# Attention scores from one fp32 copy of the queries and keys instead of fp16 halves

## The chip, the cores and the metric

One core of a Trainium2 chip runs the whole kernel. The metric is the time on the device of one execution, in microseconds (us); smaller is better. TensorE (PE) multiplies, with its weight loads recorded apart (PEld); VectorE (DVE), ScalarE (ACT) and GpSimd (POOL) do the elementwise work, and SyncE (SP) issues the DMAs.

## The reference

The reference is a decoder layer for 32 batches of 112 rows by 256 columns: attention with 8 heads of 128, a gelu block whose weights are the batch's own 375 context rows, and a quantised feed-forward block with 1024 hidden units. Each block has a layer norm in front and a residual behind. The part that changes is the scores of the attention:

```python
q = jnp.einsum('bim,mhd->bhid', x, wq)
k = jnp.einsum('bim,mhd->bhid', x, wk)
...
q = _rmsnorm(q)
k = _rmsnorm(k)
q = _rope(q)
k = _rope(k)
...
s = jnp.einsum('bhid,bhjd->bhij', q * mult, k * mult)
...
p = jax.nn.softmax(s, axis=-1)
o = jnp.einsum('bhij,bhjd->bhid', p, v)
```

## The kernel before

**Tiling.** One batch is one step of a software pipeline. All weights stay in SBUF. In step `i` each engine works on batch `a` = i (projections of q, k and v, rotary turn and norms), `b` = i-1 (scores, softmax, values, output projection), `c` = i-2 (context block and hidden units) and `d` = i-3 (the last product and the store). The order in a step is written out by hand for each engine, in the function `body` of each engine's block; every engine takes its instructions strictly in that order, and semaphores tie the engines together. The first three steps (`FIRST`, `SECOND`, `THIRD`) also split and transpose the weights, and the last three drain the pipeline.

**Precision.** Several products are made of two halves of each operand, a rounded one (`_hi`) and the rest (`_lo`): `split_products` (lines 872 to 877) issues hi times hi, hi times lo and lo times hi into one accumulation. The projections, the output projection and the context product use `F32R` halves. The scores use fp16 halves. The products of the probabilities with the values (`weigh_values`, line 937) and of the context with the normalised rows (`ctx_hidden`, line 982) take plain fp32 operands, one `pe.matmul` call each.

**The scores of batch `b`.** PE transposes the 8 heads of q and of k into PSUM (`transpose_qk`, line 917: `qT_ps` in banks 0 and 1, `kT_ps` in banks 2 and 3). ACT copies each into `qkT_hi` as fp16 (`split_qkT`, lines 710 to 713; the copy itself is recorded under line 684). DVE subtracts that copy from the same PSUM and writes `qkT_lo` (`split_qkT`, lines 548 to 552). PE waits for both `lo` copies, then makes three products of 128 by 112 by 112 a head (`scores`, lines 921 to 929, recorded under line 876). They go to `s_ps`, in banks 0 and 1 again. ACT takes the exponential (line 728), POOL masks it (line 367).

**The order around them.** On PE a step runs: transposes of q and k (b), projection of q (a, line 909), `out_units` (d, line 1013), transposes of the normalised rows `xn2` (c, line 965), scores (b), `ctx_hidden` (c, line 982), projection of k (a), transposes of the context (b, line 972; they wait for the exponential), `weigh_values` (b), `ctx_out` (c), projection of v in two halves with the transposes of the attention output between them (line 944), the transposes for the next step, then the output projection (b, line 876) with `hidden_units` (c, line 1005) between its parts. On DVE a step begins with the two subtractions, with `normalise_x2` (c, line 468) between them (behind both in the last steps), then `residual_out` (d, line 577), which waits for `out_units`. In `THIRD` there is also `split_wo(0)` (line 463) between the two subtractions. On ACT a step begins with the two copies (in `THIRD` the copy `wo_hi` stands between them), then `square_qk` (line 718).

The mapping of calls to matmul records matters below: in a trace every record on PE has its own weight load on PEld.

Of the kernel before, what the change touches and what calls it, by code (L numbers as in the profile page):

```python
# [22 lines left out]

F32 = mybir.dt.float32
F16 = mybir.dt.float16
F32R = mybir.dt.float32r
BF16 = mybir.dt.bfloat16
I16 = mybir.dt.int16
# [1 line left out]
ALU = mybir.AluOpType  # L30
AX_X = mybir.AxisListType.X

P = 128
# [35 lines left out]
def done(j):  # L69

    return j.base + j.off + 1
# [12 lines left out]
def decoder_layer(nc, x, ctx_rows, wq, wk, wv, wo, w1, b1, w2, b2, tables, out):  # L84
    B, T, M = x.shape
    S = ctx_rows.shape[1]
    _, H, D = wq.shape
# [6 lines left out]
    HH = H // 2  # L94
# [5 lines left out]
    with ExitStack() as stack:  # L100
        def sb(name, shape, dt=F32):
            return stack.enter_context(nc.sbuf_tensor(name, shape, dt))

        def sem(name):
            return stack.enter_context(nc.semaphore(name))
# [53 lines left out]
        ms = sb("ms", [T, 2, H])  # L159
        rms = sb("rms", [T, 2, H])  # L160
        qkn = sb("qkn", [T, 2, HD])
        qkT_hi = sb("qkT_hi", [P, 2, H * T], F16)
        qkT_lo = sb("qkT_lo", [P, 2, H * T], F16)
        v_sb = sb("v_sb", [T, H, VW])
        rden = sb("rden", [T, H])
        oT_hi = sb("oT_hi", [P, H, T], F32R)
# [25 lines left out]
        def bank(n, width, dt=F32):  # L192
            return psum[:, n, 0:width] if dt == F32 else psum[:, n, :].bitcast(dt)[:, 0:width]

        qT_ps, kT_ps = psum[:, 0:2, 0:HH * T], psum[:, 2:4, 0:HH * T]
        q_ps, k_ps, v_ps = psum[0:T, 4:6, :], psum[0:T, 2:4, :], psum[0:T, 0:2, :]
        s_ps = psum[0:T, 0:2, 0:HH * T]
# [26 lines left out]
            "xnT_ready", "q_ready", "k_ready", "v_ready", "qT_ready", "kT_ready", "s_ready", "o_ready"))  # L224
        oT_ready, y_ready, xn2T_ready, ctxT_ready, h_ready, ctxout_ready, xqT_ready, f_ready, f2_ready = map(sem, (
            "oT_ready", "y_ready", "xn2T_ready", "ctxT_ready", "h_ready", "ctxout_ready", "xqT_ready", "f_ready", "f2_ready"))
        xnT_hi_done, q_squared, k_squared, v_copied, qT_hi_done, kT_hi_done = map(sem, (
            "xnT_hi_done", "q_squared", "k_squared", "v_copied", "qT_hi_done", "kT_hi_done"))
        qT_lo_done, kT_lo_done = sem("qT_lo_done"), sem("kT_lo_done")
        exp_done, p_done, oT_hi_done, xn2T_copied, ctxT_copied, h_squared, tanh_done, xqT_copied, f_int_done = map(sem, (  # L230
            "exp_done", "p_done", "oT_hi_done", "xn2T_copied", "ctxT_copied", "h_squared", "tanh_done", "xqT_copied", "f_int_done"))
        stat_done = [sem(f"stat_done{n}") for n in range(3)]
# [165 lines left out]
        def _(dve):  # L398
# [18 lines left out]
            def x_rows(j):  # L417
                return 0, x_in[:, j.off % SLOTS, :], j
# [4 lines left out]
            def wait_x(j):  # L423
                dve.wait_ge(x_landed[j.off % SLOTS], landed(j))
# [41 lines left out]
            def normalise_x2(j):  # L466
                dve.wait_ge(rstd_done[1], done(j))
                dve.tensor_scalar(xn2[:, :], x2[:, j.off % 2, :], mv[1][:, 0:1], rstd[1][:, 0:1],
                                  ALU.subtract, ALU.mult).then_inc(xn2_done, 1)
# [75 lines left out]
                dve.wait_ge(xq_int_done, done(j))  # L545
                fixed(xq[:, :], xq_int[:, :]).then_inc(xq_done, 1)

            def split_qkT(w, j):
                dve.wait_ge((qT_hi_done, kT_hi_done)[w], done(j))
                dve.tensor_tensor(qkT_lo[:, w, :].rearrange("p (b n) -> p b n", b=2), (qT_ps, kT_ps)[w],  # L550
                                  qkT_hi[:, w, :].rearrange("p (b n) -> p b n", b=2),
                                  ALU.subtract).then_inc((qT_lo_done, kT_lo_done)[w], 1)

            def split_oT(n, j):
                dve.wait_ge(oT_hi_done, half(j, n))
                hs = slice(n * HH, (n + 1) * HH)
# [23 lines left out]
            def body(i):  # L580
                a, b, c, d, n, m = i, i.plus(-1), i.plus(-2), i.plus(-3), i.plus(1), i.plus(2)
                A, B_, C, D_, N, M_ = (j.inside(B) for j in (a, b, c, d, n, m))
                if i is FIRST:
                    wait_x(n)
                    layer_stats(x_rows(n))
                    normalise_x(n)
                    split_xnT(n)
                    for w in range(3):
                        split_projection(w)
                    dve.wait_ge(ident_in, 16)  # L590
                    dve.tensor_copy(ident_b[:, :], ident[:, :]).then_inc(ident_b_done, 1)
                    wait_x(m)
                    layer_stats(x_rows(m))
                    return
                if i is SECOND:
                    normalise_x(n)
                    dve.wait_ge(table_in, 32)
                    turn_cos(0, a)
                    turn_sin(0, a)
                    sum_squares(0, a).then_inc(q_summed, 1)  # L600
                    split_xnT(n)
                    turn(0, a)
                    sum_squares(1, a).then_inc(k_summed, 1)
                    turn_cos(1, a)
                    turn_sin(1, a)
                    turn(1, a)
                    normalise_k(a)
                    clip_weights(0)
                    return
                if B_:  # L610
                    split_qkT(0, b)
                if i is THIRD:
                    split_wo(0)
                if C and A:
                    normalise_x2(c)
                if B_:
                    split_qkT(1, b)
                if C and not A:
                    normalise_x2(c)
                if i is THIRD:  # L620
                    wait_x(n)
                    layer_stats(x_rows(n))
                    clip_weights(1)
                    fixed_biases()
                if D_:
                    residual_out(d)
                if A:
                    turn_cos(0, a)
                    turn_sin(0, a)
                    sum_squares(0, a).then_inc(q_summed, 1)  # L630
                if C:
                    gelu_inner(c)
                if N:
                    normalise_x(n)
                if C:
                    gelu_outer(c)
                if A:
                    turn(0, a)
                if C:
                    split_g(c)  # L640
                if A:
                    turn_cos(1, a)
                if B_:
                    invert_sums(b)
                if A:
                    turn_sin(1, a)
                if i is THIRD:
                    split_wo(1)
                if C:
                    residual_ctx(c)  # L650
                if A:
                    sum_squares(1, a, slice(0, HH))
                if B_:
                    split_oT(0, b)
                if C:
                    quantise_x3(c)
                if A:
                    sum_squares(1, a, slice(HH, H)).then_inc(k_summed, 1)
                if B_:
                    split_oT(1, b)  # L660
                if A:
                    turn(1, a)
                if N:
                    split_xnT(n)
                if A:
                    normalise_k(a)
                if B_:
                    residual_attention(b)
                if M_:
                    wait_x(m)  # L670
                if B_:
                    dve.wait_ge(x2_done, done(b))
                if B_ or M_:
                    layer_stats(*([x2_rows(b)] if B_ else []), *([x_rows(m)] if M_ else []))
                if C:
                    clip_hidden(c)
# [5 lines left out]
        def _(act):  # L682
            def copy(dst, src):
                return act.activation(dst, src, ACT.Copy)  # L684
# [22 lines left out]
                       w2T[:, :, :].rearrange("p (b c) m -> p b (c m)", b=2))[n]  # L707
                copy(dst, psum[:, 6:8, :].bitcast(BF16)).then_inc(wT_copied, 1)

            def split_qkT(w, j):  # L710
                act.wait_ge((qT_ready, kT_ready)[w], done(j))
                copy(qkT_hi[:, w, :].rearrange("p (b n) -> p b n", b=2),
                     (qT_ps, kT_ps)[w]).then_inc((qT_hi_done, kT_hi_done)[w], 1)

            def square_qk(w, j):

# [85 lines left out]
            def body(i):  # L802
                a, b, c, d, n, m = i, i.plus(-1), i.plus(-2), i.plus(-3), i.plus(1), i.plus(2)
                A, B_, C, D_, N, M_ = (j.inside(B) for j in (a, b, c, d, n, m))
# [12 lines left out]
                    round_weights(1)  # L817
                    return
                if B_:
                    split_qkT(0, b)  # L820
                if i is THIRD:
                    split_wo()
                if B_:
                    split_qkT(1, b)
                if i is THIRD:
                    copy_wT(0)
                if A:
# [43 lines left out]
        def _(pe):  # L871
            def split_products(dst, pairs, first=True, last=True):

                terms = [(lh, rh) for l, r in pairs for lh, rh in ((l[0], r[0]), (l[0], r[1]), (l[1], r[0]))]
                for k, (lh, rh) in enumerate(terms):
                    product = pe.matmul(dst, lh, rh, start=first and k == 0, stop=last and k == len(terms) - 1)  # L876
                return product
# [42 lines left out]

            def scores(j):

                pe.wait_ge(qT_lo_done, done(j))
                pe.wait_ge(kT_lo_done, done(j))
                for h in range(H):
                    at = slice(h * T, (h + 1) * T)
                    last = split_products(s_ps[:, h // HH, (h % HH) * T:(h % HH + 1) * T],
                                          [((qkT_hi[:, 1, at], qkT_lo[:, 1, at]), (qkT_hi[:, 0, at], qkT_lo[:, 0, at]))])
                last.then_inc(s_ready, 1)

            def weigh_values(j):
# [194 lines left out]
```

## Time and profile before

| what | value |
|---|---|
| time, median of 3 runs | 747.37 us |
| the runs | 747.22, 747.37, 750.02 us |
| span of the profiled execution, first to last instruction | 745.4 us |
| the profiled execution's own time | its span; no other time is listed for it |
| what the median has beyond the span | 1.97 us (0.3%) |
| PE, PEld busy | 96%, 85% |
| DVE, ACT, POOL busy | 88%, 74%, 41% |
| mean granted clock of TensorE | 0.985 of full |

A row of a group of instructions gives line, engine, operation, the tiles written and read, and the shapes. For a matmul "128*112 128x512" is a stationary operand (the weights that are loaded) of 128 rows and 112 columns, and a moving operand of 128 rows and 512 columns. Matmuls overlap in the pipeline, so the duration of one (over 200 ns) is not what it costs in a stream; the distance from one start to the next is, and so is the time that a group takes in the chain of waits divided by its count. The ends of matmuls are modelled, so small waits can hide in a PE that looks fully busy.

### The profile page before, as it was taken

How to read it: one execution, taken by the hardware profiler on the slowest of the kernel's cores; microseconds unless marked ns; L12 is line 12 of the kernel's file. 1: busy time of each engine (PE TensorE's matmuls, PEld its weight loads, DVE VectorE, ACT ScalarE, POOL GpSimd, SP SyncE). 2: the span in 40 equal slices, each digit the busy share in tenths (PEclk: the TensorE clock that was granted, in tenths of full speed). 3: DMA queues.
4: the chain of work that ended last, by engine and by line, in shares of the span. 5: the costliest groups of instructions: out<-in, count | busy, mean ns of one | idle time of the engine just before them, and what ended most of it. 6: DMA issues, size and time to landing. Idle time of an engine off the chain costs nothing.

```text
span 745.4 us, 15919 instructions
## 1 busy us (share of the span) xinstructions
PE 714.9 (96%) x5824; PEld 633.9 (85%) x5824; DVE 655.2 (88%) x1264; ACT 548.8 (74%) x1324; POOL 308.1 (41%) x425
## 2 busy tenths in 40 slices
PE   5799999999999999999999999999999999999974
PEld 4588988888888989898898989889898988889863
DVE  6989989999999999999999999999999999998942
ACT  5777777778777777787777878777787777778752
POOL 1335434543443453344344344444434444443421
PEclk9799999999999999999999999999999999999996
DMA  7400011100101100000110000101000011100000
GB/s 264 157 8 28 28 36 34 31 17 28 33 27 33 33 24 21 27 31 29 33 33 19 26 27 27 33 33 33 15 30 27 27 33 34 33 11 20 28 7 12
DMA packets 15371, 26.58 MB, mean 36 GB/s; under 512 B 1536, under 2 KB 10192, under 8 KB 15216
## 3 DMA queue, kind: packets, MB, share of 16 engines
q1 hardware_dynamic: 15344, 26.22, 10.7%
q8 instruction: 17, 0.28, 0.2%
q14 instruction: 10, 0.08, 0.0%
HBM read 22.55 MB, written 3.67 MB: 35 GB/s over the span
## 4 chain that ended last, share of the span: by engine, by line
PE 90%; DVE 3%; ACT 3%; issue 2%; DMA 1%; POOL 1%; SPq 0%; POOLq 0%; DVEq 0%; ACTq 0%
PE psum L909 34%; PE psum L876 22%; PE psum L937 7%; PE psum L917 6%; PE psum L982 6%; PE psum L1013 4%; PE psum L1005 3%; PE psum L944 3%; PE psum L972 3%; PE psum L965 2%; DMA w_raw<-in_wv 1%; ACT qkn L774 1%; ACT w_raw L764 1%; PE psum L997 1%; DVE qkT_lo L550 0%
## 5 line engine op out<-in xcount | busy, mean ns | idle before, releaser
L909 PE MATMUL psum<-wqkv_hi,xnT_hi 128*112 128x512 f32 x384 | 159.3, 415 | 4.4 <-DVE wqkv_lo L440 2.7
L909 PE MATMUL psum<-wqkv_lo,xnT_hi 128*112 128x512 f32 x384 | 151.3, 394 | 0.0
L909 PE MATMUL psum<-wqkv_hi,xnT_lo 128*112 128x512 f32 x384 | 131.8, 397 | 0.0
L344 POOL TENSOR_TENSOR rstd<-ve,nhalf 112x1 f32<-112x1 f32 x96 | 55.4, 577 | 145.8 <-DVE ve L414 140.8
L351 POOL TENSOR_TENSOR rms<-ms,nhalf 112x8 f32<-112x8 f32 x64 | 107.2, 1676 | 5.0
L718 ACT ACTIVATE sq<-psum 112x1024 f32<-112x1024 f32 x64 | 65.0, 1016 | 56.4 <-PE psum L909 56.4
L355 POOL TENSOR_TENSOR ctx_lo<-ctx_in,ctx_hi 125x768 fp32r<-125x768 f32 x32 | 58.6, 1830 | 95.9 <-ACT ctx_hi L684 95.9
L764 ACT ACTIVATE w_raw<-psum,rden 112x128 f32<-112x128 f32 x256 | 69.7, 384 | 26.6 <-DVE rden L525 26.5
L909 PEld LDWEIGHTS psum<-wqkv_hi,xnT_lo 128*112 128x112 f32 x384 | 67.3, 175 | 22.4
L909 PEld LDWEIGHTS psum<-wqkv_hi,xnT_hi 128*112 128x112 f32 x384 | 67.7, 176 | 19.8 <-issue 3.1
L774 ACT ACTIVATE qkn<-turn_c,rms 112x128 f32<-112x128 f32 x256 | 81.5, 400 | 1.4 <-POOL rms L351 1.4
L474 DVE TENSOR_REDUCE ss<-sq 112x4 f32<-112x512 f32 (+1 forms) x95 | 81.8, 861 | 0.0
L909 PEld LDWEIGHTS psum<-wqkv_lo,xnT_hi 128*112 128x112 f32 x384 | 67.9, 177 | 15.1
L482 DVE TENSOR_TENSOR turn_c<-psum,cos_t 112x1024 f32<-112x1024 f32 x64 | 77.8, 1216 | 2.2 <-ACT sq L718 2.2
L876 PE MATMUL psum<-wo_hi,oT_hi 128*112 128x256 f32 x256 | 78.8, 308 | 0.8 <-DVE oT_lo L557 0.8
L498 DVE TENSOR_TENSOR turn_c<-turn_c,turn_s 112x1024 f32<-112x1024 f32 x64 | 77.9, 1217 | 0.1
L491 DVE TENSOR_TENSOR turn_s<-psum,sin_t 112x1024 f32<-112x1024 f32 x64 | 77.3, 1208 | 0.0
L876 PE MATMUL psum<-wo_lo,oT_hi 128*112 128x256 f32 x256 | 72.1, 282 | 0.0
L876 PE MATMUL psum<-wo_hi,oT_lo 128*112 128x256 f32 x256 | 71.8, 281 | 0.0
L550 DVE TENSOR_TENSOR qkT_lo<-psum,qkT_hi 128x896 f16<-128x896 f32 x64 | 69.2, 1082 | 0.2 <-ACT qkT_hi L684 0.2
L788 ACT ACTIVATE f_int<-psum,b_col 128x112 int16<-128x112 f32 x256 | 65.9, 371 | 1.8 <-PE psum L1005 1.8
L937 PE MATMUL psum<-v_sb,w_raw 112*112 112x129 f32 x512 | 62.0, 273 | 0.0
(99 smaller groups left out, 1792.2 us busy)
## 6 DMA issues: line engine op xcount, KB each, us to landing
ctx_in<-in_ctx_rows SPq DMA_DIRECT2D x32, 375.0 KB
x_in<-in_x SPq DMA_DIRECT2D x32, 112.0 KB, 2.0
out_y<-y_out SPq DMA_DIRECT2D x32, 112.0 KB, 1.9
w_raw<-in_w SPq DMA_DIRECT2D x2, 1024.0 KB, 6.2
w_raw<-in_wq SPq DMA_DIRECT2D x2, 512.0 KB, 4.5
w_raw<-in_wk SPq DMA_DIRECT2D x2, 512.0 KB, 6.1
w_raw<-in_wv SPq DMA_DIRECT2D x2, 512.0 KB, 7.8
w_raw<-in_wo SPq DMA_DIRECT2D x1, 1024.0 KB, 10.3
```

The source lines that it names most:

```text
L351: pool.tensor_tensor(rms[:, w, :], ms[:, w, :], nhalf[:, 0:H], ALU.pow).then_inc(qk_rms_done[w], 1)
L474: return dve.tensor_reduce(ss[:, w, hs], heads(sq[:, w, :])[:, hs, :], AX_X, ALU.add)
L482: dve.tensor_tensor(turn_c[:, w, :].rearrange("t (b h d) -> t b h d", b=2, d=D), (q_ps, k_ps)[w].rearrange("t b (h d) -> t b h d", d=D), c ...
L491: dve.tensor_tensor(turn_s[:, w, :].rearrange("t (h two f) -> t h two f", two=2, f=HALF), halves, table, ALU.mult).then_inc(sin_done[w], 1)
L498: dve.tensor_tensor(turn_c[:, w, :], turn_c[:, w, :], turn_s[:, w, :], ALU.add).then_inc(qk_turned[w], 1)
L550: dve.tensor_tensor(qkT_lo[:, w, :].rearrange("p (b n) -> p b n", b=2), (qT_ps, kT_ps)[w], qkT_hi[:, w, :].rearrange("p (b n) -> p b n", b=2),
L764: last = act.activation(on[:, h * D:(h + 1) * D], o_ps[:, h // OH, (h % OH) * VW:(h % OH) * VW + D], ACT.Copy, scale=rden[:, h:h + 1])
L774: last = act.activation(qkn[:, 0, h * D:(h + 1) * D], turn_c[:, 0, h * D:(h + 1) * D], ACT.Copy, scale=rms[:, 0, h:h + 1])
L788: last = act.activation(f_int[:, c * T:(c + 1) * T], f_ps[:, c // (FC // 2), (c % (FC // 2)) * T:(c % (FC // 2) + 1) * T], ACT.Relu, bias= ...
L876: product = pe.matmul(dst, lh, rh, start=first and k == 0, stop=last and k == len(terms) - 1)
L909: last = pe.matmul(ps[:, n, :], left[:, c, :], right[:, c, w, n * BANK:(n + 1) * BANK], start=c == 0 and left is xnT_hi and right is wqkv_ ...
L937: last = pe.matmul(o_ps[:, h // OH, at:at + VW], p_sb[:, h * T:(h + 1) * T], v_sb[:, h, :], start=h % OH == 0, stop=h % OH == OH - 1 or h ...
```

## The change

The two fp16 tiles become one fp32 tile of the same size in bytes. ACT's copy writes fp32. DVE's subtractions go, and with them their semaphores; PE waits for ACT's copies instead. Each head's three fp16 products become one fp32 `pe.matmul` call. On DVE `normalise_x2` becomes the first instruction of a step.

```diff
-        qkT_hi = sb("qkT_hi", [P, 2, H * T], F16)
-        qkT_lo = sb("qkT_lo", [P, 2, H * T], F16)
+        qkT = sb("qkT", [P, 2, H * T])
...
-            def split_qkT(w, j):
-                dve.wait_ge((qT_hi_done, kT_hi_done)[w], done(j))
-                dve.tensor_tensor(qkT_lo[:, w, :].rearrange("p (b n) -> p b n", b=2), (qT_ps, kT_ps)[w],
-                                  qkT_hi[:, w, :].rearrange("p (b n) -> p b n", b=2),
-                                  ALU.subtract).then_inc((qT_lo_done, kT_lo_done)[w], 1)
...
-                if B_:
-                    split_qkT(0, b)
                 if i is THIRD:
                     split_wo(0)
-                if C and A:
-                    normalise_x2(c)
-                if B_:
-                    split_qkT(1, b)
-                if C and not A:
+                if C:
                     normalise_x2(c)
...
-            def split_qkT(w, j):
+            def copy_qkT(w, j):
                 act.wait_ge((qT_ready, kT_ready)[w], done(j))
-                copy(qkT_hi[:, w, :].rearrange("p (b n) -> p b n", b=2),
-                     (qT_ps, kT_ps)[w]).then_inc((qT_hi_done, kT_hi_done)[w], 1)
+                copy(qkT[:, w, :].rearrange("p (b n) -> p b n", b=2),
+                     (qT_ps, kT_ps)[w]).then_inc((qT_copied, kT_copied)[w], 1)
...
             def scores(j):
 
-                pe.wait_ge(qT_lo_done, done(j))
-                pe.wait_ge(kT_lo_done, done(j))
+                pe.wait_ge(qT_copied, done(j))
+                pe.wait_ge(kT_copied, done(j))
                 for h in range(H):
                     at = slice(h * T, (h + 1) * T)
-                    last = split_products(s_ps[:, h // HH, (h % HH) * T:(h % HH + 1) * T],
-                                          [((qkT_hi[:, 1, at], qkT_lo[:, 1, at]), (qkT_hi[:, 0, at], qkT_lo[:, 0, at]))])
+                    last = pe.matmul(s_ps[:, h // HH, (h % HH) * T:(h % HH + 1) * T],
+                                     qkT[:, 1, at], qkT[:, 0, at], start=True, stop=True)
                 last.then_inc(s_ready, 1)
```

## Rows read from the trace of the kernel before

**Rows 1.** The page's first part: engine, busy us (share of the span), instructions.

```profile
PE 714.9 (96%) x5824; PEld 633.9 (85%) x5824; DVE 655.2 (88%) x1264; ACT 548.8 (74%) x1324; POOL 308.1 (41%) x425
```

**Rows 2.** Stretches: length, PE, PEld, DVE, ACT, POOL busy (count), PE clock, DMA, GB/s.

```profile
0.00:56.00 56.00, 42.06 (x264) 34.36 (x265) 44.45 (x68) 38.61 (x59) 15.02 (x29) 0.91 0.40 143
56.00:699.00 643.00, 643.00 (x5312) 574.36 (x5311) 589.41 (x1145) 487.47 (x1204) 281.12 (x381) 1.00 0.09 28
699.00:745.40 46.40, 29.82 (x253) 25.20 (x251) 21.35 (x53) 22.70 (x63) 11.96 (x16) 0.86 0.03 8
```

**Rows 3.** The chain that ended last, one period: start us, us, what.

```profile
360.44 1.24 PE psum L876 x24
361.68 1.36 PE psum L982 x12
...
366.47 1.77 PE psum L937 x16
...
376.92 1.53 PE psum L917 x16
...
382.31 1.24 PE psum L876 x24
```

**Rows 4.** Groups on PE and DVE: shapes, count, busy us, mean ns, idle before.

```profile
L937 PE MATMUL psum<-v_sb,w_raw 112*112 112x129 f32 x512 | 62.0, 273 | 0.0
L917 PE MATMUL psum<-ident,qkn 112*128 112x112 f32 x512 | 56.2, 263 | 2.6 <-ACT qkn L774 2.2 <-DVE qkn L503 0.3
L982 PE MATMUL psum<-xn2T,ctxT 128*125 128x112 f32 x384 | 48.7, 277 | 1.6 <-issue 1.6
...
L550 DVE TENSOR_TENSOR qkT_lo<-psum,qkT_hi 128x896 f16<-128x896 f32 x64 | 69.2, 1082 | 0.2 <-ACT qkT_hi L684 0.2
```

**Rows 5.** Timeline around one batch's scores (ACT, DVE, PE): start us, us, instruction.

```profile
377.72 1.76 ACT L684 ACTIVATE qkT_hi<-psum 128x896 f16<-128x896 f32 x2
380.32 1.08 DVE L550 TENSOR_TENSOR qkT_lo<-psum,qkT_hi 128x896 f16<-128x896 f32 x1
382.16 0.42 DVE L577 SCALAR_TENSOR_TENSOR y_out<-psum,x3b 112x256 f32<-112x256 f32 x1 [0.76 <-PE psum L1013]
381.95 0.36 PE L965 MATMUL psum<-ident,xn 112*128 112x112 f32 x2
382.15 0.21 PE L876 MATMUL psum<-qkT_hi 128*112 128x112 f16 x1
383.59 0.92 ACT L728 ACTIVATE w_raw<-psum 112x896 f32<-112x896 f32 x1
```

**Rows 6.** An fp32 copy on ACT: count, shortest, median, longest ns.

```profile
L684 ACT ACTIVATE ctxT<-psum x32: 778/790/791, 40.5 to 715.5; 128x750 f32<-128x750 f32 x32
```

**Rows 7.** Timeline of the first scores (PE, ACT).

```profile
27.87 1.73 PE L917 MATMUL psum<-ident,qkn 112*128 112x112 f32 x8 [0.35 <-DVE qkn L503]
29.39 1.91 PE L885 MATMUL psum<-ident_b,w_raw 128*128 128x128 bf16 x16
32.68 0.31 PE L876 MATMUL psum<-qkT_hi 128*112 128x112 f16 x1 [1.38 <-DVE qkT_lo L550]
34.94 1.75 PE L895 MATMUL psum<-ident_b,w_raw 128*128 128x128 bf16 x16
30.18 0.91 ACT L684 ACTIVATE qkT_hi<-psum 128x896 f16<-128x896 f32 x1
```

**Rows 8.** Stretches around the first scores, columns as in rows 2.

```profile
30.00:34.00 4.00, 2.62 (x27) 2.38 (x25) 3.61 (x9) 3.75 (x4) 0.75 (x2) 0.50 0.00 0
34.00:38.00 4.00, 4.00 (x36) 3.67 (x35) 3.97 (x7) 2.34 (x3) 1.50 (x3) 0.71 0.02 4
```

**Rows 9.** Timeline of the last scores (PE, ACT).

```profile
706.52 1.08 PE L1013 MATMUL psum<-w2T,f_q 128*112 128x256 bf16 x8 [0.19 <-DVE f_q L564]
708.79 0.23 PE L876 MATMUL psum<-qkT_hi 128*112 128x112 f16 x1 [1.19 <-DVE qkT_lo L550]
705.52 1.78 ACT L684 ACTIVATE qkT_hi<-psum 128x896 f16<-128x896 f32 x2
```

More of the change, by code:

```diff
@@ L24 @@
 F32 = mybir.dt.float32
-F16 = mybir.dt.float16
 F32R = mybir.dt.float32r
@@ L226, in decoder_layer @@
             "oT_ready", "y_ready", "xn2T_ready", "ctxT_ready", "h_ready", "ctxout_ready", "xqT_ready", "f_ready", "f2_ready"))
-        xnT_hi_done, q_squared, k_squared, v_copied, qT_hi_done, kT_hi_done = map(sem, (
-            "xnT_hi_done", "q_squared", "k_squared", "v_copied", "qT_hi_done", "kT_hi_done"))
-        qT_lo_done, kT_lo_done = sem("qT_lo_done"), sem("kT_lo_done")
+        xnT_hi_done, q_squared, k_squared, v_copied, qT_copied, kT_copied = map(sem, (
+            "xnT_hi_done", "q_squared", "k_squared", "v_copied", "qT_copied", "kT_copied"))
         exp_done, p_done, oT_hi_done, xn2T_copied, ctxT_copied, h_squared, tanh_done, xqT_copied, f_int_done = map(sem, (
@@ L819, in body @@
                 if B_:
-                    split_qkT(0, b)
+                    copy_qkT(0, b)
                 if i is THIRD:
@@ L823, in body @@
                 if B_:
-                    split_qkT(1, b)
+                    copy_qkT(1, b)
                 if i is THIRD:
```

## The prediction

> **What bounds the kernel now.** I read the busy shares first: PE 96% and DVE 88% [rows 1]. Either could be the bound, and the change takes work from one and alters it on the other, so the shares alone decide nothing. I then cut the span into three stretches [rows 2]. From 56 to 699 us PE is busy for 643.00 of 643.00 us at the full granted clock (1.00, the level of 2.4 GHz), while DVE is busy for 589 of them; before and after, PE has gaps (42 of 56 us, 30 of 46 us). The chain of waits says the same: in one period every link is PE work, and the scores of one batch begin 382.31 - 360.44 = 21.87 us after those of the batch before [rows 3]. So in the middle a microsecond on PE is a microsecond of the total, and a microsecond taken from DVE is worth nothing as long as PE doesn't wait for it. Because matmul ends are modelled, I checked the one place where a wait for DVE could hide. The two transposes ahead of the scores start at 381.95 and the scores at 382.15 [rows 5]: 0.10 us each, as transposes cost anywhere (1.53 / 16 = 0.096 us [rows 3]). No wait is hidden there.
>
> **The change, part by part.** The sum is made against the profiled execution, whose only listed time is its span of 745.4 us; the median of the runs is 1.97 us above it, and I add the difference to the median.
>
> *The products.* Taken away: 24 fp16 products a batch, 1.24 us in the chain, 51.7 ns each [rows 3]. Added: 8 fp32 calls. How many records is a call? `weigh_values` makes 8 calls a batch, 256 in all, and has 512 records; `ctx_hidden` makes 6, 192 in all, and has 384 [rows 4]. So a plain fp32 product is two records, each with its own weight load; only transposes (512 calls, 512 records of line 917) are one. That gives 16 records in place of 24.
>
> No row has this record, 112 stationary by 112 moving columns in fp32, so I bound it. From below: the fp32 transposes, the same 112 moving columns, 1.53 / 16 = 95.6 ns. From above: `ctx_hidden`, the same moving columns but 125 stationary ones, 1.36 / 12 = 113.3 ns [rows 3]. Nearer rows by scaling: `weigh_values`, 112 stationary and 129 moving columns, costs 1.77 / 16 = 110.6 ns, times 112/129 is 96.0; `ctx_hidden` times 112/125 is 101.5. Their middle is 98.7 ns, which I take, since the new product ties the two widths that bind one in each row. So 16 x 98.7 = 1.58 us, and the batch pays 1.58 - 1.24 = 0.34 us more. The ends give 1.53 and 1.81 us, or +0.29 and +0.57.
>
> What the rows show is that a pair of fp32 records costs about 2 x 98.7 = 197 ns where three fp16 ones cost 155. The Trainium skill has a rule that also speaks against the change ("FP8 and Floating Point Precision", section "TensorE Precision Notes"): true fp32 takes four passes through the array. Four passes at the row's 51.7 ns would be an estimate of 207 ns a head, 1.65 us a batch, +0.41, and a total of about 758.5 us instead of mine; the rows have two records per call and 2 x 95.6 to 2 x 113.3 ns for them, so the trace neither needs nor excludes it.
>
> *DVE's subtractions.* 64 instructions of 1.08 us, 69.2 us in all [rows 4], 2.16 us a batch. In the middle they cost nothing now: `residual_out` right behind them waits 0.76 us for PE's `out_units` [rows 5]. Without them DVE reaches that wait some 2 us earlier and stands there longer; what follows it starts when PE allows, as now. Gain in the middle: 0. `normalise_x2` moves forward by about 1 us, to no effect, since its reader on PE comes later in PE's own order.
>
> *The wait of the scores.* It passes from DVE's second subtraction (ends 381.40) to ACT's second copy (ends 379.48), 2.7 us before the scores begin at 382.15 [rows 5]. That cover would have to go entirely before PE stood still. The two copies take 1.76 us now [rows 5]. ACT's nearest fp32 copy from PSUM moves 750 columns in 790 ns [rows 6]: two of 896 columns cost at least 2 x 0.79 = 1.58 us, and 2 x 0.79 x 896/750 = 1.89 us with nothing of it fixed. So the copies end between 0.18 us sooner and 0.13 us later, I take no change, and ACT's queue keeps its order. No DMA and no queue of SP or POOL is touched.
>
> *What comes after.* The exponential starts when the scores end (383.59, [rows 5]) and shifts by 0.34 us, but so does all that PE does after them; the transposes that need it stand behind `ctx_hidden` and the projection of k on PE, as before. No new wait.
>
> *The edges.* Twice PE does wait for the subtraction. At the first scores it stands idle 1.38 us; ACT's copy of k ends at 30.18 + 0.91 = 31.09 and the weight transposes ahead of the scores at 31.30, so the wait goes [rows 7]. But the clock is at 0.50 there, the level of 1.2 GHz, after gaps on PE, and comes back only while PE runs on (0.71 over 34 to 38 us) [rows 8]. The fp16 scores took 34.94 - 32.68 = 2.26 us; a transpose cost (29.39 - 27.87) / 8 = 0.19 us at that clock [rows 7], times 98.7/95.6 and 16 is 3.14. Net: -1.38 + 0.88 = -0.50 us. At the last scores PE stands idle 1.19 us; ACT's copies end at 707.30 and `out_units` at 707.60 [rows 9], so the scores start at 707.60 and last 0.34 longer: -0.85 us. The work behind both is released by these scores and moves along. Together -1.35.
>
> *Sum.* 30 batches in the middle at +0.342 are +10.26; the edges give back 1.35; +8.9 us. On the median: 747.4 + 8.9 = **756.3 us**.
>
> **The rivals.**
> *The stationary side binds.* If a record costs what `ctx_hidden` shows, 113.3 ns, each batch pays +0.573, 30 of them 17.2, the edges give back some 0.7: 763.9 us. For it: that product is the closest in kind. Against: it has 125 columns to load, and `weigh_values` with 112 scales to 96.0.
> *One record a head (the other side).* If the call became one record, as a transpose does, a batch would take 8 x 95.6 = 0.76 us, -0.48; 30 of them -14.2, edges -2.1 and -1.7: 729 us. The place is PE's stream of scores, the price 95.6 ns a record, and it turns the sign below 1.24 / 0.0956 = 13 records a batch. Against: both plain fp32 products have two records a call [rows 4].
> *DVE's relief pays.* If a good part of PE's 21.87 us a period were waits for DVE hidden under modelled ends, 2.16 us less on DVE could win more than the 0.34 lost; half of it would give 30 x (0.34 - 1.08) - 1.35 = -23.6, 724 us. It decides from 0.34 us of hidden wait a batch. For it: DVE at 88%. Against: DVE itself waits for PE each batch, and the starts ahead of the scores leave no room [rows 5].
> *No difference.* A record at 77.3 ns (1.24 / 16) would break even: 746 us with the edges. No fp32 row is below 95.6.
>
> **How the numbers follow.** Chances: the forecast 0.80, the stationary side 0.12, one record 0.03, the relief 0.02, no difference 0.03. The range runs from the lower bound of the record with the first scores at full clock (30 x 0.29 - 1.38 - 0.73 - 0.90 = +5.7, 753.1) to the upper one (763.9); I set it from 752.5 to 764, a little beyond, for the scatter of the runs. A measurement here can tell about 0.5%, 3.7 us, from no change. Both ends are slower by more: slower 0.92, same 0.03, faster 0.05.
>
> **What would show it.** Right: 512 fp32 records of the scores; a period of about 22.2 us in the chain, still all PE; the scores' link 1.53 to 1.65 us with 16 records; DVE busy some 69 us less, its idle time ahead of `residual_out` up by about 2 us a batch; no idle PE ahead of the first and the last scores; the clock at 1.00 throughout the middle. Wrong: 256 records; a period at or under 21.87 us; a link of DVE or ACT in the middle of the chain; or ACT copies that end over 2.7 us later against PE's work.

## The result and the profile after

The changed kernel took 754.32 us (median of 4 runs, 753.48 to 755.38) against 747.3 us (4 runs, 747.21 to 750.02): a ratio of 1.0091, 95% interval 1.007 to 1.0113. It is slower, by 7.0 us or 0.9%; the forecast was 756.3, range 752.5 to 764. The span of the profiled execution went from 745.4 to 751.8 us, +6.4; that execution took 753.57 us, 1.77 beyond its span.

First the page's shares of the changed kernel, to be held against [rows 1]:

```profile
PE 723.0 (96%) x5568; PEld 642.1 (85%) x5568; DVE 597.2 (79%) x1200; ACT 552.0 (73%) x1324; POOL 306.8 (41%) x425
```

DVE lost 58.0 us of busy time and 64 instructions, PE gained 8.1 us with 256 instructions fewer. The stretches say where (columns as in [rows 2]):

```profile
0.00:56.00 56.00, 42.62 (x253) 34.92 (x254) 41.23 (x65) 39.20 (x59) 15.65 (x30) 0.94 0.41 143
56.00:705.00 649.00, 649.00 (x5063) 580.61 (x5063) 534.69 (x1080) 488.49 (x1198) 279.15 (x380) 1.00 0.09 28
705.00:751.80 46.80, 31.41 (x256) 26.59 (x254) 21.25 (x57) 24.34 (x70) 12.03 (x16) 0.88 0.03 8
```

The middle is still PE without a gap at the full granted clock, and DVE now has 114 us to spare there. The chain of waits in the middle, to be read beside [rows 3] (`scores` is now line 912, `ctx_hidden` 967):

```profile
363.65 1.57 PE psum L912 x16
365.22 1.31 PE psum L967 x12
...
385.81 1.57 PE psum L912 x16
```

The scores' link is 1.57 us with 16 records in place of 1.24 with 24, `ctx_hidden` behind it is 1.31 in place of 1.36, and the period is 385.81 - 363.65 = 22.16 us in place of 21.87: +0.29 a batch. The group of the scores counts the records, two for each of 256 calls:

```profile
L912 PE MATMUL psum<-qkT 128*112 128x112 f32 x512 | 56.2, 264 | 0.1
```

What DVE was freed of turned into waiting, as its longest waits show (total us, times, longest; before, 24.5 us and 0.7 us stood in these two lines):

```profile
DVE y_out L568 <- PE psum L998: 64.8, 30, 2.4
...
DVE xn L465 <- POOL rstd L341: 17.6, 32, 0.8
```

At the two ends PE's idle time ahead of the scores is gone in this execution. The timeline around the first scores (with ACT's copy of k ahead of them) and the last, beside [rows 7] and [rows 9]:

```profile
28.91 1.73 PE L902 MATMUL psum<-ident,qkn 112*128 112x112 f32 x8 [0.20 <-DVE qkn L500]
30.43 1.91 PE L870 MATMUL psum<-ident_b,w_raw 128*128 128x128 bf16 x16
31.36 0.91 ACT L669 ACTIVATE qkT<-psum 128x896 f32<-128x896 f32 x1
32.41 2.38 PE L912 MATMUL psum<-qkT 128*112 128x112 f32 x16
34.63 1.15 PE L880 MATMUL psum<-ident_b,w_raw 128*128 128x128 bf16 x16
...
714.41 1.08 PE L998 MATMUL psum<-w2T,f_q 128*112 128x256 bf16 x8 [0.19 <-DVE f_q L555]
715.34 1.80 PE L912 MATMUL psum<-qkT 128*112 128x112 f32 x16
```

In the drain behind the last scores the clock falls. A stretch of 5 us that begins 20.2 us behind the start of the last scores, in the kernel before and then in the changed one (columns as in [rows 2]):

```profile
729.00:734.00 5.00, 1.81 (x10) 1.61 (x9) 1.52 (x3) 1.42 (x3) 1.05 (x1) 0.87 0.00 0
735.50:740.50 5.00, 1.81 (x14) 1.41 (x12) 1.52 (x3) 1.42 (x3) 1.47 (x1) 0.97 0.01 3
```

### The profile page after: what moved, and what is told of

The parts are those of the page before. It is cut to its first block, busy times and chain, and to the rows that moved or that the text cites. A ratio compares the mean times of both kernels' runs of the same rounds, so it can differ in the third digit from the quotient of the medians.

```text
span 751.8 us, 15337 instructions
## 1 busy us (share of the span) xinstructions
PE 723.0 (96%) x5568; PEld 642.1 (85%) x5568; DVE 597.2 (79%) x1200; ACT 552.0 (73%) x1324; POOL 306.8 (41%) x425
## 4 chain that ended last, share of the span: by engine, by line
PE 90%; DVE 4%; ACT 2%; issue 2%; DMA 1%; POOL 0%; SPq 0%; POOLq 0%; DVEq 0%
PE psum L894 33%; PE psum L861 16%; PE psum L922 7%; PE psum L912 6%; PE psum L902 6%; PE psum L967 5%; PE psum L998 4%; PE psum L990 3%; PE psum L929 3%; PE psum L957 3%; PE psum L950 2%; DMA w_raw<-in_wv 1%; DVE turn_c L495 1%; DVE turn_c L479 1%; ACT w_raw L749 1%
## 5 line engine op out<-in xcount | busy, mean ns | idle before, releaser
L568 DVE SCALAR_TENSOR_TENSOR y_out<-psum,x3b 112x256 f32<-112x256 f32 x32 | 13.6, 424 | 64.8 <-PE psum L998 64.8
```

## The experiments

The theory: PE's stream of records sets the whole difference, a record costs about 98 ns, and the two waits at the ends give a little back. The rivals: DVE's relief changes the middle too; one side of the product alone sets the record's price; the price is fixed per record.

**DVE's subtractions put back.** The products stay fp32, DVE subtracts as before, and PE waits for it.

```diff
+        qkT_lo = sb("qkT_lo", [P, 2, H * T], mybir.dt.float16)
...
-                pe.wait_ge(qT_copied, done(j))
-                pe.wait_ge(kT_copied, done(j))
+                pe.wait_ge(qT_lo_done, done(j))
+                pe.wait_ge(kT_lo_done, done(j))
...
```

> The fp32 products, but DVE keeps both subtractions (into a tile that nobody reads) and PE waits for them, as in the kernel before. If PE's stream of scores alone sets the difference: the period in the middle stays at 22.16 us and the link of ctx_hidden at 1.31 us (it got 0.05 us shorter because fp32 now follows fp32), while about 1.3 us of idle PE comes back ahead of the first and of the last scores, so the span is 1.0 to 2.0 us above the changed kernel's 751.8. If DVE's relief paid in the middle: the ctx_hidden link returns to 1.36 us and the period rises by 0.05 us or more, so the span is over 753.8 us.

Measured: 756.63 us, a ratio of 1.0127 (1.0093 to 1.016), span 754.5. The chain in the middle, then the stretch from 56 to 706 us:

```profile
364.92 1.57 PE psum L926 x16
366.49 1.31 PE psum L981 x12
...
387.08 1.57 PE psum L926 x16
```

```profile
56.00:706.00 650.00, 650.00 (x5073) 581.62 (x5072) 591.34 (x1139) 489.44 (x1198) 279.65 (x380) 1.00 0.09 28
```

DVE has its 591 us of work again and neither the period (22.16) nor the `ctx_hidden` link (1.31) moved. DVE's relief is worth nothing in the middle. The ends are another matter:

```profile
32.70 3.30 PE L926 MATMUL psum<-qkT 128*112 128x112 f32 x16 [1.45 <-DVE qkT_lo L549]
35.79 1.34 PE L894 MATMUL psum<-ident_b,w_raw 128*128 128x128 bf16 x16
...
717.96 1.80 PE L926 MATMUL psum<-qkT 128*112 128x112 f32 x16 [1.19 <-DVE qkT_lo L549]
```

Both idle times are back. The span rose by 2.7 us (the median by 2.3), over the 1.0 to 2.0 expected of the theory and past the 753.8 us named for its rival. The rival's own marks, a longer period and a `ctx_hidden` link of 1.36, did not come: from the start to the second scores the run is 1.2 us behind the changed kernel, and in the period ahead of the last scores 1.35. Part of the first is the clock: the first scores took 35.79 - 32.70 = 3.09 us against 34.63 - 32.41 = 2.22 in the changed kernel, so the low clock held through most of them here. The clock there is 0.50 over 30 to 34 us in this run and 0.54 in the changed kernel, but 0.72 against 1.00 over 34 to 38 us.

**Every product made twice.**

```diff
-                    last = pe.matmul(s_ps[:, h // HH, (h % HH) * T:(h % HH + 1) * T],
-                                     qkT[:, 1, at], qkT[:, 0, at], start=True, stop=True)
+                    for _ in range(2):
+                        last = pe.matmul(s_ps[:, h // HH, (h % HH) * T:(h % HH + 1) * T],
+                                         qkT[:, 1, at], qkT[:, 0, at], start=True, stop=True)
```

> Every fp32 product of the scores is made twice, 32 records a batch in place of 16, the second over the first. If a record's price is what the stream shows (98.2 ns from start to start) and nothing hides it: the period rises by 16 x 0.098 = 1.57 us to 23.73 us and the span by about 50 us to 802 us. If part of the 1.57 us link is paid once per group, for the switch from transposes: less, down to 16 x 0.0956 = 1.53 us a batch. If PE has slack against another engine: much less.

Measured: 804.25 us, span 802.5. The chain:

```profile
362.98 3.15 PE psum L913 x32
...
386.71 3.15 PE psum L913 x32
```

The period is 23.73 us, +1.57 for 16 records: 98 ns each, all of it on the path. Nothing of the link is paid once per group.

**Narrower operands.** Three runs cut 112 columns to 96: the stationary operand (keys), the moving one (queries), both. The edit shown is that of the third; the other two make one half of it each.

```diff
-                    last = pe.matmul(s_ps[:, h // HH, (h % HH) * T:(h % HH + 1) * T],
-                                     qkT[:, 1, at], qkT[:, 0, at], start=True, stop=True)
+                    last = pe.matmul(s_ps[0:96, h // HH, (h % HH) * T:(h % HH) * T + 96],
+                                     qkT[:, 1, h * T:h * T + 96], qkT[:, 0, h * T:h * T + 96], start=True, stop=True)
```

> The stationary operand of each score product has 96 columns in place of 112, the moving one still 112; the last 16 keys of each head are left out. If the wider of the two sides binds a record: the moving side still has 112, so the record costs 96 to 98 ns and the period stays between 22.12 and 22.16 us. If the stationary side (the weight load) sets the price: 98.2 x 96/112 = 84 ns, and the period falls by 0.22 us to 21.94 us.

> The moving operand of each score product has 96 columns in place of 112, the stationary one still 112; the last 16 queries of each head are left out. If the wider side binds: the stationary side has 112, the record costs 98 to 101 ns and the period stays between 22.16 and 22.21 us. If the moving side alone sets the price: 84 ns and a period of 21.94 us.

> Both operands of each score product have 96 columns in place of 112; the last 16 keys and queries of each head are left out. If the columns set the price, on whichever side: 16 x 84 ns = 1.35 us a batch and a period of 21.94 us. If a fixed price per record sets it: 22.16 us as with 112.

Measured in this order: 751.53, 755.96 and 746.18 us, one run each. The chain of the run with 96 stationary columns, then 96 moving, then both:

```profile
361.45 1.53 PE psum L912 x16
...
383.57 1.54 PE psum L912 x16
```

```profile
363.93 1.56 PE psum L912 x16
...
386.09 1.56 PE psum L912 x16
```

```profile
359.71 1.36 PE psum L912 x16
...
381.66 1.36 PE psum L912 x16
```

Periods of 22.12, 22.16 and 21.95 us. Cutting either side alone saves next to nothing (95.6 and 97.5 ns a record); cutting both gives 85 ns. So the wider of the two binds in these products, at 0.85 to 0.89 ns a column, and the two rivals of one side alone, and of a fixed price, fall.

The run with 96 stationary columns also shows something of the first scores. Its program is the changed kernel's up to there, but its clock was 1.00 from 26 to 34 us, where the changed kernel's was 0.60 and then 0.54, and its first scores do wait, for ACT's copy of k:

```profile
31.03 1.75 PE L912 MATMUL psum<-qkT 128*96 128x112 f32 x16 [1.41 <-ACT qkT L669]
```

On ACT the copy `wo_hi` (1.9 us) stands ahead of the copy of k. In the changed kernel's profiled execution the weight transposes, 1.91 us long at the low clock and 1.06 at the full one, cover that copy, which ends at 32.27.

**One F32R product a head.** The copy is rounded to F32R; the remainders of both operands are left out.

```diff
-        qkT = sb("qkT", [P, 2, H * T])
+        qkT = sb("qkT", [P, 2, H * T], F32R)
```

> The one copy is rounded to F32R and each head's score is one F32R product of the rounded operands, so the remainders of both are left out. It has 8 records a batch in place of 16, each with 4-byte operands. If the load of a 4-byte stationary operand binds at 112 columns: a record still costs about 98 ns, 8 of them 0.79 us, and the period falls by 0.79 to 21.37 us. If the price follows the moving columns at the rate of the F32R projections (232 ns for 512): about 51 ns, 0.41 us, and a period of 21.00 us.

Measured: 730.31 us (one run), span 728.6. The chain:

```profile
353.14 0.74 PE psum L912 x8
353.88 1.36 PE psum L967 x12
...
374.51 0.74 PE psum L912 x8
```

The period is 374.51 - 353.14 = 21.37 us, the value expected if a record still costs about 98 ns: 0.79 us less than 22.16 for 8 records less. The moving side alone, at the F32R projections' rate, would have given 21.00. With 112 columns on both sides an F32R call has half the records of an fp32 call, and each costs as much; that the load of the 4-byte stationary operand is what binds is not shown: no run separates it from the moving side for F32R.

**One fp16 product a head.** The copy is fp16; the fp16 remainders are left out, and DVE makes no subtraction.

```diff
-        qkT = sb("qkT", [P, 2, H * T])
+        qkT = sb("qkT", [P, 2, H * T], mybir.dt.float16)
```

> The one copy is fp16 and each head's score is one fp16 product, so the fp16 remainders of both operands are left out; DVE makes no subtraction. 8 fp16 records of 51.6 ns in place of 16 fp32 ones: the link falls from 1.57 to 0.41 us, the period from 22.16 to about 21.00 us, the span by some 36 us to about 716 us. If DVE or ACT bound the kernel just below PE: a period above 21.1 us with links of DVE or ACT in the middle of the chain.

Measured: 728.58 us, a ratio of 0.974 (0.9716 to 0.9764), span 727.0 and not 716. The chain ("issue" is time in which the engine waited for nothing that the profile shows), then a line of the waits in the middle, then the timeline:

```profile
372.96 0.41 PE psum L912 x8
373.37 0.08 issue
373.45 1.53 PE psum L967 x12
...
394.24 0.41 PE psum L912 x8
```

```profile
PEld psum L967 <- DVE y_out L568: 5.3, 29, 0.2
```

```profile
372.80 0.43 DVE L568 SCALAR_TENSOR_TENSOR y_out<-psum,x3b 112x256 f32<-112x256 f32 x1 [2.03 <-PE psum L998]
372.99 0.36 ACT L669 ACTIVATE xn2T<-psum 128x224 f32<-128x224 f32 x1
```

The link is 0.41 us as expected, but the period is 21.28 us here and not 21.00. The gap stands at `ctx_hidden`, which waits for two things: DVE's `y_out` must have read `out_units` from the bank that it overwrites, and ACT must have copied `xn2T`. The line of the waits names `y_out`, but that ended at 373.23 and the copy at 373.35, and `ctx_hidden` started 0.10 us behind the copy, at 373.45; in each of 27 batches in the middle the copy is the last to end. The copy stands behind ACT's square of q (1.02 us), and 0.41 us of scores no longer cover the two. Without the copy `y_out` would be next, 0.12 us earlier, so moving one of them alone can win back little. A stretch of work that is shortened stops hiding what ran beside it.

**`out_units` earlier.** As the last, but `out_units` is issued between the two halves of the projection of q.

```diff
-                    project(0, a, q_ps, q_ready)
+                    project(0, a, q_ps, q_ready, only=0)
+                    if D_:
+                        out_units(d)
+                    project(0, a, q_ps, q_ready, only=1)
...
```

> As the run with one fp16 product a head (the fp16 remainders of both operands are left out), and out_units is issued on PE between the two halves of the projection of q instead of behind both, 1.4 us earlier. If PE's wait ahead of ctx_hidden comes from DVE's y_out, which needs out_units and is hidden by the scores where they are long: the wait goes, and the period falls from 21.30 to 21.0 to 21.1 us, the span by 6 to 9 us from 727.0. If it comes from the copy of xn2T on ACT or from the scores themselves: the period stays at 21.30 us. If DVE's f_q is not ready that early: a wait ahead of out_units takes its place.

Measured: 748.13 us, a ratio of 1.0009 to the kernel before (0.9996 to 1.0022). A miss: the wait ahead of `ctx_hidden` grew and the period became 382.05 - 360.06 = 21.99 us.

```profile
360.06 0.41 PE psum L912 x8
...
382.05 0.41 PE psum L912 x8
382.47 0.80 issue
383.27 1.53 PE psum L967 x12
```

```profile
382.82 0.35 ACT L669 ACTIVATE xn2T<-psum 128x224 f32<-128x224 f32 x1
```

The edit brought `y_out` forward, which was not what `ctx_hidden` waited for (it ended at 380.93, 2.3 us ahead of it), and put off what it did wait for: the projection of q now ends 0.87 us nearer to `ctx_hidden`, and ACT squares q (1.0 us) ahead of the copy of `xn2T`. The copy ends at 383.17, and `ctx_hidden` starts 0.10 us behind it again.

**That copy first.** As the run before it, with ACT's copy of `xn2T` ahead of squaring q.

```diff
+                if C and A:
+                    copy_xn2T(c)
                 if A:
                     square_qk(0, a)
...
```

> As the run before it (one fp16 product a head, the fp16 remainders left out; out_units between the halves of the projection of q), but ACT copies xn2T ahead of squaring q. If the 0.8 us wait ahead of ctx_hidden in that run came from ACT's squaring, which starts when the later-ending projection of q is done and stands ahead of the copy of xn2T: the wait goes, and the period falls from 22.00 us to 21.0 to 21.1 us, also under the 21.30 us of one fp16 product a head in the old order, since y_out is no longer late; the span is about 718 to 721 us. If what ctx_hidden waits for is neither, the period stays at 21.3 us or more.

Measured: 760.67 us, a ratio of 1.0187 (1.0165 to 1.0209). A second miss: the wait ahead of `ctx_hidden` is down to 0.2 us (5.1 us in 28 times), which shows that ACT's order had made it, but the period is 22.4 us, for the chain now leaves PE:

```profile
367.28 1.03 ACT sq L703
368.33 1.23 DVE turn_c L479
...
374.41 0.43 DVE g_lo L527
374.88 1.31 PE psum L864 x9
```

The later end of q's projection holds ACT's square, that holds DVE's turn of q, and DVE, in strict order, reaches `g_lo` late for `ctx_out`. With less work on PE the order of the other engines is the limit; whether another order reaches 21.0 us was not tried.

**fp32 at the two ends only.** The halves of fp16 stay in batches 1 to 30; the first and the last batch take the fp32 copy and product. Nothing is left out.

```diff
+        def edge(j):
+            return isinstance(j.base, int) and j.base + j.off in (0, B - 1)
...
+                    if edge(j):
+                        last = pe.matmul(s_ps[:, h // HH, (h % HH) * T:(h % HH + 1) * T],
+                                         qkT[:, 1, at], qkT[:, 0, at], start=True, stop=True)
+                        continue
```

> The kernel before, with its fp16 halves in batches 1 to 30, and the fp32 copy and products in the first and the last batch alone (the fp32 tile lies in the same bytes as the halves). If the edges give back what the two traces show: the period is 21.87 us in the middle and the span 1.5 to 3 us below the kernel before, 742.4 to 743.9 us, a ratio of 0.996 to 0.998. If the gain at the edges belongs to DVE's relief in the steps around them and not to the wait of these two batches: no gain, 745 us or more.

Measured: 744.48 us, a ratio of 0.9953 (0.9935 to 0.9972), span 743.4: the span expected, with a ratio a little below the 0.996 to 0.998. It is faster than both kernels with no product left out. The chain in the middle, then the first and the last scores:

```profile
359.10 1.24 PE psum L882 x24
360.34 1.36 PE psum L996 x12
...
380.97 1.24 PE psum L882 x24
```

```profile
32.06 1.80 PE L938 MATMUL psum<-qkT 128*112 128x112 f32 x16 [1.42 <-ACT qkT L690]
...
705.18 1.08 PE L1027 MATMUL psum<-w2T,f_q 128*112 128x256 bf16 x8 [0.19 <-DVE f_q L570]
706.10 1.80 PE L938 MATMUL psum<-qkT 128*112 128x112 f32 x16
```

The period is 21.87 again, and the last scores follow `out_units` without a gap. How much of the 2.0 us between the spans belongs to the first batch can't be read from this run: its clock was already 0.95 over 26 to 30 us, and its first scores waited 1.42 us after all, for ACT's copy of k in place of DVE's subtraction.

## Why the prediction was right, point by point

- **PE binds the middle, DVE's relief is worth nothing there.** Right: 649.00 of 649.00 us busy, and the run with the subtractions put back has the same period. What the prediction did not say is that a part of DVE's free time, 17.6 us, goes into `normalise_x2` waiting for POOL's root, since it now comes first in the step; it costs nothing. So the wait ahead of `residual_out` grew by 40.3 us, some 1.3 a batch, where 2 were named. DVE's busy time fell by 58.0 us and not by 69: its records, added up one by one, fell by 67.8, but neighbouring ones overlap, which busy time counts once.
- **Two records a call, 98.7 ns each.** Right: 512 records, and 98 ns by the doubled products. Scaling by the width was sound: the narrower operands show that the wider side binds, and here both are 112. The bound of 113.3 belonged to a product of 125 columns that also paid for what stood ahead of it: its records start 109 ns apart but for one step (last section), and 109 x 112/125 is 97.8, not 101.5. That the middle of 96.0 and 101.5 came out at 98.7 is in part luck, since one end was too low and the other too high. The Trainium skill's four passes ("FP8 and Floating Point Precision", section "TensorE Precision Notes"), priced at the fp16 row, would have been an estimate of 1.65 us a batch; the trace has 1.57, in two records.
- **+0.34 us a batch.** The term that was mis-sized: +0.29. The scores' own link grew by 0.33, as forecast, but the link of `ctx_hidden` shrank by 0.05, which no step had. Over 30 batches that is 1.5 us (`ctx_hidden` is the subject of the last section).
- **The edges, -1.35 us.** The two waits were read rightly, the size was not, and part of what came out is luck. Taking 30 periods of +0.293 (8.8 us) from the +6.4 of the span leaves -2.4.
  - *The start.* The second scores came 0.77 us earlier than before (53.24 and 54.01 us), and the period behind them grew by only 0.15; forecast -0.50. Two things cross here. The first scores took 2.22 us and not the 3.14 priced at the low clock, and the transposes behind them 35.59 - 34.63 = 0.96 us against 36.49 - 34.94 = 1.55: the clock came back sooner (1.00 over 34 to 38 us, 0.71 in [rows 8]). But the transposes of k ahead of them began 1.04 us later than before (28.91 and 27.87), ahead of anything that the change touches. In the run with 96 stationary columns, the same program up to there, they began at 27.77, so this is scatter of the start.
  - *The idle time ahead of the first scores.* In this execution it went while the clock was low (0.60 and 0.54), and that is luck. In two runs at the full clock the first scores waited 1.41 and 1.42 us for ACT's copy.
  - *The end.* The last scores began 0.93 us behind the start of `out_units` in place of 2.27 and lasted 0.37 us longer: -0.97, forecast -0.85. Another 0.5 us came in the drain, where the clock fell later (0.97 against 0.87) and the nine products of the last `ctx_out` took 1.42 us in place of 1.92. The change does not touch that product.
- **The sum.** +8.9 forecast, +7.0 between the medians, +6.4 between the spans; the two terms above make up the difference to the spans: 1.5 + 1.0. The profiled execution of the changed kernel is one of the two shorter of its four (753.5 and 753.6 us; the others took 755.1 and 755.4), so the 1.0 holds some scatter too.
- **The rivals.** One record a head and no difference fell with the record count and the period. The stationary side at 113.3 ns fell with the 98 ns measured; that this side alone doesn't set the price is shown by the run with 96 stationary columns (95.6 ns and not 84).

## What to carry to other kernels

Price a new product by counting the records of the same kind of call in the trace and by the distance between their starts, scaled by the wider operand (a record that stands first behind another kind has a step of its own, so take the starts inside the group); three fp16 products at 112 columns (155 ns) cost less here than one fp32 product (196 ns). Work taken from an engine that another one waits for only twice in a run pays twice, not 32 times, so look in which steps the wait really ends on it, and who comes next: at the first scores ACT's copy took DVE's place wherever the clock was full. When the binding engine is relieved, ask at once what the removed time was covering: the run with one fp16 product gained 18.8 us on the kernel before, where 16 records of 51.7 ns less in each of 32 batches promised 26. Where an instruction waits for two engines, compare the ends of both with its start before one is moved: the line of the waits named DVE, and ACT's copy was what ended last.

## What the runs showed of the hardware that was not expected

- The group behind fp16 products pays for it: `ctx_hidden` took 1.36 us behind fp16 products (before, and in the run with fp32 at the ends only) and 1.31 behind fp32 ones, with or without DVE's subtractions. It took 1.36 behind F32R products too, so it is not the 2-byte type alone. Read record by record in the trace, all of it stands between the group's first matmul and its second: 156 ns behind fp16 and 152 behind F32R, where every other step, and every step behind fp32 products of 112 columns, is 109. Why that one step is longer stays open.
- An fp32 product's record gets cheaper only when both its sides get narrower (95.6 and 97.5 ns with one side at 96 columns, 85 with both); an F32R record at 112 by 112 lowered the period by the same 98 ns a record that an fp32 record adds.
- The clock at the first scores isn't the same from run to run. Over 26 to 30 us it was 0.60 in the changed kernel and 1.00 in the run with 96 stationary columns, the same program up to there; over 34 to 38 us it was 0.71 in the kernel before, 1.00 in the changed one and 0.72 with the subtractions put back. The first scores took 2.22 us in the changed kernel and 3.09 with the subtractions put back.
